# Moving the small jobs of a selective-scan and FFN block to other places in the engines' queues

## The reference, cut to what matters

```
xz = x @ W_xproj.T;  dt_raw, Bm, Cm = xz[:64], xz[64:80], xz[80:96]
dt = softplus(dt_raw @ W_dt.T + b_dt)
for each token t, for each of 16 states s, 256 channels:
    h[s] = exp(dt * A[s]) * h[s] + (dt * x) * Bm[s]
    y   += h[s] * Cm[s]
x1  = layernorm(x + y + Dp * x)
out = layernorm(x1 + (silu(x1 @ Wg.T) * (x1 @ Wu.T)) @ Wd.T)      # hidden 768
```

## Time and profile before

| | |
|---|---|
| median of 3 runs | 1930.44 us (1929.3 to 1931.55) |
| the profiled execution: its own time, span | 1934.14 us, 1932.4 us |
| granted PE clock, mean | 0.982 |
| busy: DVE, PE, POOL, ACT | 1715.8 (89%), 1692.2 (88%), 1641.3 (85%), 1586.5 (82%) |
| POOL times_c (L408), times_b (L398) | 352 of 2368 ns, 320 of 2370 ns |
| DVE scans (L699) | 1024 of 1209 to 1271 ns |

### The profile page before, as it was taken

How to read it: one execution, slowest core, us unless ns; L and a number is a source line. 1 busy time by engine, 2 the same in 40 slices (tenths; PEclk the granted TensorE clock), 3 DMA queues, 4 the chain that set the end, 5 groups by cost and what they waited for, 6 DMA issues and landing times. The chain is left out here.

```text
span 1932.4 us, 33150 instructions
## 1 busy us (share of the span) xinstructions
PE 1692.2 (88%) x11048; PEld 1347.9 (70%) x11048; DVE 1715.8 (89%) x2060; ACT 1586.5 (82%) x2992; POOL 1641.3 (85%) x710
## 2 busy tenths in 40 slices
PE   6788989988989888989888989888989888989877
PEld 4676777776777766777666777766777666777755
DVE  4888999999899898999999899998999999899993
ACT  6779888888888889888888888888888888888863
POOL 5988898988898988988988898988988988898960
PEclk7999999999999999999999999999999999999989
DMA  7322443223443223444233444223444233433200
GB/s 250 96 98 84 138 136 129 92 88 108 138 133 133 88 85 115 138 133 132 87 91 111 138 133 131 86 86 119 138 133 131 83 91 116 138 133 121 67 12 22
DMA packets 107419, 216.51 MB, mean 112 GB/s; under 512 B 10129, under 2 KB 44530, under 8 KB 107250
## 3 DMA queue, kind: packets, MB, share of 16 engines
q1 hardware_dynamic: 107250, 214.39, 34.6%
HBM read 195.48 MB, written 18.87 MB: 111 GB/s over the span
## 5 line engine op out<-in xcount | busy, mean ns | idle before, releaser
L408 POOL TENSOR_TENSOR h<-h,c_bc 128x1024 f32<-128x1024 f32 x352 | 830.3, 2368 | 114.4 <-DVE h L699 60.5
L398 POOL TENSOR_TENSOR ub<-u,b_bc 128x1024 f32<-128x1024 f32 x320 | 753.9, 2370 | 0.1
L922 PE MATMUL p_y<-ident,h 128*128 128x128 f32 x4096 | 522.7, 277 | 30.9 <-POOL h L408 29.5
L504 ACT ACTIVATE p_da<-dt,neg_a 128x512 f32<-128x512 f32 x640 | 435.2, 683 | 137.1 <-DVE h L699 133.4
L922 PEld LDWEIGHTS p_y<-ident,h 128*128 128x128 f32 x4096 | 473.6, 143 | 77.5 <-POOL h L408 38.3
L699 DVE TENSOR_TENSOR_SCAN h<-p_da,h_carry,ub 128x512 f32<-128x512 f32 x320 | 394.9, 1269 | 19.0 <-ACT p_da L504 19.0
L699 DVE TENSOR_TENSOR_SCAN h<-p_da,ub 128x512 f32<-128x512 f32 x320 | 376.2, 1209 | 26.6 <-ACT p_da L504 21.7
L518 ACT ACTIVATE ub_t<-u_t,bc_t 128x256 f32<-128x256 f32 x768 | 345.8, 499 | 0.0
L977 PE MATMUL p_o<-wt_down,hid 128*128 128x256 f32 x1536 | 342.5, 379 | 2.4 <-DVE res L740 1.6
L977 PEld LDWEIGHTS p_o<-wt_down,hid 128*128 128x128 f32 x1536 | 289.0, 190 | 54.6 <-issue 14.7
L504 ACT ACTIVATE da_k<-dt,neg_a 128x512 f32<-128x512 f32 x384 | 267.8, 714 | 0.0
(11 more groups left out here) (91 smaller groups left out, 1643.0 us busy)
## 6 DMA issues: line engine op xcount, KB each, us to landing
c_bc<-bc_rows_dram SPq DMA_DIRECT2D x352, 256.0 KB, 6.4
b_bc<-bc_rows_dram SPq DMA_DIRECT2D x64, 768.0 KB, 6.6
b_bc<-bc_rows_dram SPq DMA_DIRECT2D x64, 512.0 KB, 4.0
x_in<-in_L_attn_x SPq DMA_DIRECT2D x32, 512.0 KB, 6.2
out_x<-res_n SPq DMA_DIRECT2D x32, 512.0 KB, 3.3
bc_rows_dram<-bc_rows SPq DMA_DIRECT2D x32, 64.0 KB, 1.7
hid<-in_L_ffn_w_gate SPq DMA_DIRECT2D x1, 768.0 KB, 5.1
hid<-in_L_ffn_w_up SPq DMA_DIRECT2D x1, 768.0 KB, 6.9
```

The costliest lines, as they stand in the source:

```text
L398: nc.gpsimd.tensor_tensor(ub[:, i % UB_SLOTS, :, :], u[:, par, :, :], b_bc[:, i:i + 1, :].broadcast_to([P, DH, T]), ALU.mult).then_inc(s_u ...
L408: nc.gpsimd.tensor_tensor(h[:, s % H_SLOTS, :, :], h[:, s % H_SLOTS, :, :], c_bc[:, i:i + 1, :].broadcast_to([P, DH, T]), ALU.mult).then_i ...
L504: nc.scalar.activation(da, dt[:, par, q, :], ACT.Exp, scale=neg_a[:, q, s:s + 1]).then_inc(done, 1)
L922: ins = nc.tensor.matmul(p_y_tok[:, k, q * P:(q + 1) * P], h[:, s % H_SLOTS, q, k * P:(k + 1) * P], ident[:, :], start=(s == SUM_ORDER[0] ...
```

## The change

Only two tables change: 57 of the 74 places in `AT`, and `DA_LEAD`. No instruction is added or removed and no wait is rewritten; the order within the queues changes, and with it what waits behind what.

```diff
-    "weights": (7, 1), "x_transposed": (1, 3), "x_out": (1, 3), "project": (2, 1), "rank_out": (3, 2),
-    "bc_out": (3, 1), "project_dt": (3, 2), "softplus_abs": (4, 3), "softplus_exp": (5, 1),
-    "softplus_log": (6, 1), "dt_of": (6, 2), "u_of": (5, 1), "u_transposed0": (11, 4), "u_out0": (14, 0),
-    "u_transposed1": (14, 3), "u_out1": (15, 1), "z_out": (2, 3), "stats1": (3, 1), "mean1": (5, 2),
-    "norm_log": (5, 2), "norm_exp": (5, 3), "shifts": (6, 1), "norm1_0": (6, 1), "norm1_1": (6, 2),
-    "norm1_2": (6, 3), "norm1_3": (7, 1), "x1_transposed": (7, 1), "x1_high": (7, 3), "x1_low": (9, 0),
-    "gate0": (9, 2), "gate1": (9, 2), "gate2": (9, 4), "gate3": (9, 4), "gate4": (10, 1), "gate5": (10, 1),
-    "silu0": (9, 0), "silu1": (9, 1), "silu2": (9, 1), "silu3": (9, 1), "silu4": (9, 3), "silu5": (10, 1),
-    "exp_table": (10, 1), "up0": (10, 1), "up1": (11, 0), "up2": (11, 1), "up3": (13, 2), "up4": (13, 4),
-    "up5": (14, 1), "hidden0": (10, 2), "hidden1": (12, 2), "hidden2": (13, 1), "hidden3": (13, 2),
-    "hidden4": (15, 0), "hidden5": (15, 0), "skip0": (7, 1), "skip1": (6, 2), "down0": (1, 0), "down1": (1, 1),
-    "down2": (1, 1), "down3": (1, 2), "down4": (3, 1), "down5": (3, 1), "down6": (3, 1), "down7": (3, 2),
-    "residual0": (1, 1), "residual1": (4, 1), "stats2": (5, 0), "mean2": (5, 2), "norm2_0": (9, 2),
-    "norm2_1": (11, 2), "norm2_2": (14, 1), "norm2_3": (15, 3), "bc_turned": (6, 1), "bc_cols": (11, 1),
+    "weights": (7, 1), "x_transposed": (0, 4), "x_out": (0, 2), "project": (2, 1), "rank_out": (4, 0),
+    "bc_out": (3, 1), "project_dt": (3, 3), "softplus_abs": (5, 1), "softplus_exp": (5, 1),
+    "softplus_log": (5, 3), "dt_of": (7, 0), "u_of": (7, 0), "u_transposed0": (12, 2), "u_out0": (14, 0),
+    "u_transposed1": (14, 3), "u_out1": (14, 2), "z_out": (2, 0), "stats1": (4, 0), "mean1": (5, 1),
+    "norm_log": (6, 0), "norm_exp": (6, 0), "shifts": (6, 1), "norm1_0": (6, 2), "norm1_1": (7, 1),
+    "norm1_2": (7, 1), "norm1_3": (7, 1), "x1_transposed": (8, 0), "x1_high": (8, 0), "x1_low": (8, 2),
+    "gate0": (9, 3), "gate1": (9, 3), "gate2": (10, 1), "gate3": (10, 2), "gate4": (10, 2), "gate5": (10, 2),
+    "silu0": (9, 1), "silu1": (9, 1), "silu2": (9, 2), "silu3": (10, 0), "silu4": (10, 0), "silu5": (10, 0),
+    "exp_table": (10, 0), "up0": (10, 2), "up1": (10, 2), "up2": (13, 0), "up3": (13, 1), "up4": (13, 4),
+    "up5": (14, 3), "hidden0": (11, 0), "hidden1": (11, 0), "hidden2": (13, 1), "hidden3": (14, 0),
+    "hidden4": (15, 0), "hidden5": (15, 0), "skip0": (8, 2), "skip1": (6, 1), "down0": (0, 3), "down1": (1, 0),
+    "down2": (1, 0), "down3": (1, 2), "down4": (2, 4), "down5": (2, 4), "down6": (3, 0), "down7": (3, 2),
+    "residual0": (1, 2), "residual1": (4, 2), "stats2": (5, 1), "mean2": (5, 2), "norm2_0": (11, 1),
+    "norm2_1": (11, 2), "norm2_2": (14, 3), "norm2_3": (15, 1), "bc_turned": (6, 0), "bc_cols": (9, 2),
 }
...
-DA_LEAD = {6: 2, 10: 2, 14: 2, 15: 2}
+DA_LEAD = {6: 2, 9: 3, 10: 2, 14: 2}
```

## The result

| | before | after |
|---|---|---|
| median (runs) | 1930.99 us (4) | 1904.97 us (1902.89 to 1905.66, 4) |
| profiled execution, span | 1934.14, 1932.4 us | 1904.62, 1902.8 us |
| pair of chunks 16 and 17 | 116.05 us | 114.09 us |

The ratio of the times is 0.9863, interval 0.9842 to 0.9883: 1.4% faster, clear of the noise. The prediction was 1937 us, slower, with a range that began at 1906; it was wrong in sign. All medians here are of fast executions; one slow execution of gate2_early (4023.51 us) is left out of its median.

A forecast was written before the change was run, and what follows sets the result against it. It took a chain through DVE with small gaps as the bound. Even 58.02 plus odd 58.5 made a pair 116.5 against 116.05 us; with small items +7, so 1937 us, own range 1920 to 1953, wider range 1906 to 1956.

The forecast's parts named there:

- the rule of rows 4 to 6: DVE's `shifts` stays held by the SBUF port lock across POOL hand-overs; seen in holds of 0.60 and 5.00 us.
- A: Mark on DVE: scan 6, q=1, right behind `shifts`; forecast 23.50 us into even chunks, 23.2 into odd.
- Rival 1: `shifts` gets through when times_b 8 ends or isn't held; 4.5 us less a pair, 1870 us; chance 0.15.
- the odd 23.2: Odd chunk, start to `shifts`' end: ten POOL instructions to the end of times_c 4, 23.2 us, 1.10 later.
- carry 0 at 4.55: Even chunk: with x_out now ahead of it, carry 0 starts 4.55 us into the chunk, before 3.64.
- A to S: From A to scan 11, q=0, first behind the silus: ACT's queue, 19.37 us even, 19.8 odd (1.38, 0.9 less).
- S to the end: From scan 11, q=0, first behind the silus, to the chunk's end: 15.15 us even, 15.5 odd.
- hidden0's wait: DVE's wait of hidden0 for up0 stays at 1.5 to 2 us, done while DVE's next scan waits for its decay.
- rival 2: POOL's string in even chunks is not held by carry 0; 1.2 us earlier there, 1918 us; chance 0.05.
- Rival 3: PE's clock falls after idling while DVE is held, x1's transposes slow; 14 us more, 1950 us; chance 0.08.
- start to A: From the chunk's first scan to A: 23.50 us even, 23.2 odd, 2.15 and 1.10 later than before.
- state 9's decays at 0.62 us: On ACT behind A, before the first silu: one decay of state 9 less, 0.68 less 0.06 us.

The follow-up runs named there:

- gate2_early: Changed kernel with gate2 back ahead of the second transposes of state 10: 1911.98 us.
- shift_scalar: Changed kernel with `shifts` as eight `tensor_scalar`, each with one SBUF tensor and rstd as a scalar: 1892.02 us.
- before_uof_late: Kernel before the change with only `u_of` moved behind times_c 4: 1963.36 us.
- split_only: Changed kernel with `shifts` as four `tensor_scalar` at the old place and four behind scan 10: 1875.57 us.
- lead9_back: Changed kernel without the earlier decays of state 9 (back at state 8): 1932.71 us.
- u_of_behind_b11: Changed kernel with `u_of` one place later on POOL, behind times_b 11: 1938.3 us.
- b11_broken_later: Changed kernel with `u_of` behind times_b 11, a wait ahead of times_b 7 in odd chunks and a 0.27 us memset ahead of `shifts`: 1908.85 us.
- after_again: The changed kernel again, no edit: 1905.32 us.
- pool_late: Changed kernel in which POOL also waits for `mean2` ahead of times_b 8: 1898.31 us.
- shifts_late: Changed kernel with a 0.27 us memset on DVE ahead of `shifts`: 1906.32 us.
- pool_after_log: Changed kernel in which POOL, in even chunks only, starts times_b 8 when log_var is there: 1931.68 us.
- u_of_b11_broken: Changed kernel with `u_of` behind times_b 11 and, in odd chunks, a POOL wait for state 4's scan ahead of times_b 7: 1872.89 us.
- b11_shifts_later: Changed kernel with `u_of` behind times_b 11 and a 0.91 us memset ahead of `shifts`: 1959.33 us.

## Why the prediction was wrong

**The step that failed** is "So `shifts` meets a POOL that goes on from times_b 8 to times_c 4, and waits for the end of times_c 4, if the rule of rows 4 to 6 holds", in its even half. Two holds, in chunk 1 and the last chunk, were made a rule for 30 others, and only the one of 5.00 us had passed a hand-over: the one of 0.60 us ended where POOL's string itself ended. The trace of the kernel before held no middle chunk in which `shifts` met a hand-over; those two were not a sample of the rest. In the even chunks `shifts` took 0.48 us and was done with times_b 8, so A came at 21.13 and not at 23.50: 2.37 us in each of 15, 36 us in all. Rival 1 said what happened, for even chunks; its 1870 counted a gain in odd chunks too. These got none, because `shifts` came 0.32 us into times_c 4 there, and not, as rival 1 assumed, within times_b 8. So the odd 23.2 of the forecast came true (23.04) without a test of its rule, which is luck. Neither the forecast nor the rival had walked DVE's arrival against POOL's place in each kind of chunk; with both walked, the mixed case (even let in, odd held, about 1905) would have stood between them.

**What held.** That `shifts`' wait for POOL is a cost of the right size where it happens (shift_scalar, before_uof_late); carry 0 at 4.55 in the even chunk (4.54); A to S through ACT's queue (19.37 against 19.39, 19.8 against 19.81); S to the end; that hidden0's wait is slack. POOL's string is held by carry 0, 1.20 us at 942.42, so rival 2 is out.

**Rival 3 did happen, and cost next to nothing.** The mean granted clock (0.984, before 0.982) hides it. Behind PE's wait of 2.9 us the state sums take 2.9 to 3.4 us instead of 1.91 in eight of the 14 middle odd chunks of the changed kernel, at a granted clock between 0.50 and 0.72 from 2.5 to 5.0 us behind A (1.00 is the 2.4 GHz level, 0.50 the 1.2 GHz level, and what lies between is a stretch with both), and x1's transposes start up to 1.4 us later. A to S is 19.81 there too, so this stretch had the slack; in the last chunk it is 21.01. Chunk 19, and the last chunk:

```profile
1132.87:1135.37 2.50, 2.48 (x15) 2.50 (x16) 2.50 (x3) 2.50 (x7) 1.41 (x1) 0.64 0.05 11
1820.42:1822.92 2.50, 2.47 (x12) 2.50 (x13) 2.50 (x3) 2.50 (x7) 0.10 (x1) 0.50 0.01 3
```

In gate2_early the same fall is not hidden (20.06 to 20.17). In split_only, where the hold is gone, PE waits for 1.4 to 1.6 us there, and the granted clock in the 8 us from 1 us behind A is 1.00 in every chunk but the last (0.91).

**Where the gain came from.** A to S gave 1.36 and 0.89 us, S to the end 0.07 and 0.36; start to A gave 0.22 and took 0.94. The forecast had these gains and buried them under a hold of 2.4 us in each even chunk. Its working of A to S counted state 9's decays at 0.62 us, as work moved away; lead9_back shows 0.97 us, since they also filled a wait for a scan.

**What decides who gets in is not settled.** Refuted as the sole cause: the wait for `h_carry` ahead of times_c 4, the form of the scan or operation ahead, and the moment of arrival. For a long unbroken run of POOL as a condition speak the last pair in u_of_behind_b11 and b11_broken_later (15 in a row: passed over; 4: let in, with the same arrival), and that in after_again, pool_late, shifts_late and pool_after_log those let in at a hand-over stand behind 7 or fewer and those passed over behind 15 or more. Against it as the whole rule: the last chunk of before_uof_late was let in behind 11, where the last chunk of the kernel before was passed over behind 11; chunk 1 of u_of_behind_b11 was let in behind 10, with a pause of 0.12 us ahead of them; in the last chunks of u_of_b11_broken and b11_broken_later `shifts` got through behind 15; and the even chunks of b11_shifts_later ran inside a times_c. The last chunk also weakens the pair itself: there the added wait ahead of times_b 7 shows no pause, the arrival is the same (0.03 us into times_c 4 against 0.02 in u_of_behind_b11, 0.30 against 0.32 in shifts_late), and yet the two kernels with the wait let `shifts` through (0.14 and 2.09 us) and the two without it pass it over (4.66 and 4.38 us). So it may be the wait's being in POOL's queue rather than the pause; no run separates the two. The Trainium skill (SBUF — State Buffer, section "SBUF: two separate sides") has the lock go to whoever starts first, for one whole instruction. The even chunks (0.48 us, ended with times_b 8) agree; the 4.38 us over a hand-over and the 0.10 us within a POOL instruction do not, and here the measurement decides.

## What to carry to other kernels

A tiny DVE operation with two SBUF tensors beside a busy POOL can cost 0.1 to 7.4 us, and which of these it costs can change with one more wait elsewhere: give it a scalar operand and one SBUF tensor (split_only, 1875.6 us), rather than reason about its place. When a rule rests on two rare cases, ask first what makes them differ from the common case, and give the mixed outcome a chance. Price an early decay by the wait that it fills as well as by its own length. Look at all chunks, not at one pair: what the clock did, and what gate2_early cost, shows in some odd chunks only.

## What was not expected of the hardware

- A DVE `tensor_scalar` on one element a partition takes about 0.13 us in a row (eight in 1.05 us), so eight of them cost more than the lock did in even chunks.
- The function table load (1.28 us) is followed at once by the first silu (969.63 to 970.92), as ACT after shows:

```profile
969.63 1.28 ACT L538 ACT_TABLE_LOAD   x1
970.92 1.08 ACT L538 ACTIVATE hid<-p_m 128x512 f32<-128x512 f32 x2
```

- The same wait of PE lets the granted clock fall in some chunks and not in others. Behind 2.9 us it fell in eight of the 14 middle odd chunks of the changed kernel and in nine of gate2_early, and stayed at 1.00 in the rest, as in chunk 17 of the changed kernel:

```profile
1018.80:1021.30 2.50, 2.37 (x20) 2.16 (x20) 2.50 (x3) 2.50 (x7) 1.40 (x1) 1.00 0.03 10
```
